# The channel products of a four-layer convolution kernel: one row per matmul on 64 partitions, in place of block-diagonal weights

## What is computed

```
layer 0:  q = x as (8, 64, 65536); att = q q^T; x = gamma * (softmax(max(att) - att) q) + x
layer 1:  x = conv2d(x, k1, separable 256x256 kernel per channel) + x * bias1
layer 2:  f1 = haar2d(x)
          for i in 0, 1:
              f4 = einsum('bchw,oc->bohw', f1 * v[i], conv_w[i])
              acc += sign(f4) * relu(|f4| - tau[i])
          x = haar2d_inverse(acc) + x
layer 3:  x = conv2d(x, k3) + x * bias3
```

## Time and profile before

| | |
|---|---|
| median of 3 runs | 6836.3 us (6832.41 to 6836.76) |
| the profiled execution's own time | 6835.24 us |
| its span in the trace | 6833.4 us |
| TensorE busy | 6388.9 us, 93% |
| VectorE, ScalarE, GpSimd busy | 65%, 58%, 39% |
| channel stage, eight times | about 240 us each, some 28% of the span |

### The profile page before, as it was taken

One profiled execution on the slowest core, in us unless ns is written; L12 is line 12 of the kernel. 1 busy time (PEld: TensorE's weight loads), 2 busy tenths in 40 slices (PEclk: granted clock), 3 DMA queues, 4 the chain that ended last, 5 costly groups with the idle time before them and its releaser, 6 DMA issues.

```text
span 6833.4 us, 144168 instructions
## 1 busy us (share of the span) xinstructions
PE 6388.9 (93%) x41056; PEld 5800.8 (85%) x41056; DVE 4433.1 (65%) x7037; ACT 3968.3 (58%) x5913; POOL 2698.2 (39%) x2052
## 2 busy tenths in 40 slices
PE   8998999889998899988999889998899988999689
PEld 7987999779997799977999779997799977998579
DVE  3667646676566764677646776567765677656766
ACT  1568545675456754567545775457654576545865
POOL 0149311483115831167311673117631176311852
PEclk9999999999999999999999999999999999999999
DMA  6654666546664466644666446664466644665236
GB/s 222 126 139 138 123 168 132 141 129 130 169 132 141 126 130 167 132 146 122 131 167 132 147 121 131 167 132 145 122 130 169 131 149 119 131 173 125 80 86 129
DMA packets 621293, 944.27 MB, mean 138 GB/s; under 512 B 62358, under 2 KB 456759, under 8 KB 621208
## 3 DMA queue, kind: packets, MB, share of 16 engines
q1 hardware_dynamic: 547480, 808.74, 51.3%
q10 hardware_dynamic: 73728, 134.25, 5.3%
HBM read 673.92 MB, written 268.83 MB: 138 GB/s over the span
## 4 chain that ended last, share of the span: by engine, by line
PE 75%; DVE 10%; ACT 8%; issue 3%; DMA 2%; POOL 1%; DVEq 1%; SPq 0%; ACTq 0%; POOLq 0%
PE ps L359 26%; PE ps L361 13%; PE ps L387 7%; PE ps L379 7%; PE ps L464 7%; PE ps L416 7%; PE ps L370 6%; DVE work L767 4%; DVE ps L782 4%; ACT ps L601 4%; ACT mag L598 4%; DMA work<-in_x_pix 1%; POOL mag L844 1%; PE ps L337 1%; DMA coef<-work 0%
## 5 line engine op out<-in xcount | busy, mean ns | idle before, releaser
L359 PE MATMUL ps<-work 128*128 128x256 f32 x8192 | 2455.2, 382 | 23.9 <-POOL work L833 16.3
L361 PEld LDWEIGHTS ps<-work 128*128 128x128 f32 x8192 | 1561.8, 191 | 214.3
L361 PE MATMUL ps<-work 128*128 128x128 f32 x8192 | 1578.0, 274 | 0.0
L359 PEld LDWEIGHTS ps<-work 128*128 128x128 f32 x8192 | 1315.8, 192 | 121.5 <-issue 20.7
L833 POOL COPY work<-field 128x512 f32 (+1 forms) x512 | 312.8, 614 | 2308.6 <-DVE ps L731 1623.3
L844 POOL TENSOR_TENSOR mag<-mag,sgn 128x1024 f32<-128x1024 f32 x512 | 1091.8, 2132 | 331.9 <-ACT mag L598 315.6
L862 POOL TENSOR_TENSOR split_a<-field,split_a 128x512 fp32r<-128x512 f32 x512 | 650.8, 1271 | 1418.8 <-ACT split_a L616 1418.8
L782 DVE TENSOR_TENSOR ps<-ps,tau_t 128x1024 f32<-128x1024 f32 x512 | 631.2, 1233 | 313.0 <-ACT ps L601 313.0
L569 ACT ACTIVATE work<-ps 128x512 f32<-128x512 f32 x512 | 306.1, 598 | 874.0 <-PE ps L361 871.1
L616 ACT ACTIVATE split_a<-field 128x512 fp32r (+1 forms) x512 | 322.9, 631 | 698.9 <-PE ps L379 694.6
L767 DVE TENSOR_TENSOR work<-ps,v_t 128x1024 f32<-128x1024 f32 x512 | 622.3, 1215 | 92.9 <-PE ps L464 92.9
(11 more groups left out here) (76 smaller groups left out, 9942.9 us busy)
## 6 DMA issues: line engine op xcount, KB each, us to landing
work<-filt SPq DMA_DIRECT2D x2048, 128.0 KB, 4.0
work<-in_x_pix SPq DMA_DIRECT2D x256, 512.0 KB, 5.4
coef<-work ACTq DMA_DIRECT2D x512, 256.0 KB, 2.1
out<-work SPq DMA_DIRECT2D x512, 256.0 KB, 4.1
rows<-in_x_rows SPq DMA_DIRECT2D x128, 512.0 KB, 4.4
mag<-in_x_rows SPq DMA_DIRECT2D x128, 512.0 KB, 4.4
rows<-coef SPq DMA_DIRECT2D x128, 512.0 KB, 3.6
split_a<-coef SPq DMA_DIRECT2D x64, 512.0 KB, 3.7
```

Source lines behind the costliest of these rows:

```text
L359: nc.tensor.matmul(o_ps, src[:, 0, H * half:H * half + H], tab[:, N - 1::-1], start=True, stop=False)
L361: mm = nc.tensor.matmul(o_ps[:, H:N], src[:, 1, H * half:H * half + H], tab[:, N - 1:H - 1:-1], start=False, stop=True)
```

## The change

The weights are no longer block-diagonal: `chan_w` holds the 64 x 128 weights twice, in partitions 0 to 63 and 64 to 127. The partitions of a chunk are ordered (s, c) in place of (c, s), so a matmul takes the 64 partitions of one half and 128 moving columns; there are eight of them in a unit, the lower and the upper half in turn, and half s writes bank 2(d%2)+s. The transposes write their columns in the new order; the tables `v` and `tau`, their views on VectorE, and the views of GpSimd's addition follow the new order of the banks. What each engine computes per unit is otherwise the same.

```diff
-        chan_w = sb("chan_w", [128, 4 * C])
+        chan_w = sb("chan_w", [128, 2 * C])
...
-                chunks = coef.rearrange("c (s t) n -> (c s) (t n)", s=2)
+                chunks = coef.rearrange("c (s t) n -> s c (t n)", s=2)
...
-                    sp.dma_start(crows[buf], chunks[:, bass.ds(1024 * k, 1024)]).then_inc(crows_in[buf], 16)
+                    sp.dma_start(crows[buf], chunks[:, :, bass.ds(1024 * k, 1024)]).then_inc(crows_in[buf], 16)
...
                     for a in range(2):
-                        o_ps = ps[:, 2 * (d % 2) + a, :].rearrange("p (i c h) -> p i c h", i=2, h=4)
                         for t in range(2):
                             at = 512 * t + N * a + H * (d % 2)
-                            mm = nc.tensor.matmul(o_ps[:, :, :, 2 * t:2 * t + 2], src[:, at:at + H], chan_w[:, :],
-                                                  start=True, stop=True)
+                            for s in range(2):
+                                o_ps = ps[:, 2 * (d % 2) + s, :].rearrange("p (a n t) -> p a n t", a=2, t=2)
+                                mm = nc.tensor.matmul(o_ps[:, a, :, t], src[C * s:C * s + C, at:at + H],
+                                                      chan_w[C * s:C * s + C, :], start=True, stop=True)
...
-                            mm = nc.tensor.transpose(o_ps[:, :, 2 * t:2 * t + 2], src[:, at:at + H], eye[:, :])
+                            turned = o_ps[:, :, 2 * t:2 * t + 2].rearrange("p c s -> p s c")
+                            mm = nc.tensor.transpose(turned, src[:, at:at + H], eye[:, :])
...
-                        at = t[:, j % 2, bass.ds(2 * q + j // 2, 1), :].rearrange("p o (x h) -> p (o x) h", h=4)
-                        return at.unsqueeze(2).to_broadcast([128, 4, C, 4])
+                        at = t[:, j % 2, bass.ds(2 * q + j // 2, 1), :].rearrange("p o (x h) -> p (o x) h", h=2)
+                        return at.unsqueeze(2).to_broadcast([128, 8, C, 2])
...
-                        both = mag[:, d].rearrange("p (a i n) -> p a i n", a=2, i=2)
-                        nc.gpsimd.tensor_tensor(pair_sum[:, d].rearrange("p (a n) -> p a n", a=2),
-                                                both[:, :, 0, :], both[:, :, 1, :], ALU.add)\
+                        both = mag[:, d].rearrange("p (s a i n) -> p s a i n", s=2, a=2, i=2)
+                        nc.gpsimd.tensor_tensor(pair_sum[:, d].rearrange("p (a n s) -> p s a n", a=2, s=2),
+                                                both[:, :, :, 0, :], both[:, :, :, 1, :], ALU.add)\
```

More of the change, by code:

```diff
@@ L766, in shrink @@
                         dve.wait_ge(c_sign, u - 1 + CR)
-                        nc.vector.tensor_tensor(held[:, j % 2].rearrange(grouped, x=4, h=4),
-                                                banks(j % 2).rearrange(grouped, x=4, h=4), table(v_t), ALU.mult)\
+                        nc.vector.tensor_tensor(held[:, j % 2].rearrange(grouped, x=8, h=2),
+                                                banks(j % 2).rearrange(grouped, x=8, h=2), table(v_t), ALU.mult)\
                             .then_inc(c_scaled, 1)
@@ L779, in shrink @@
                     if on[0]:
-                        less = banks(j % 2).rearrange(grouped, x=4, h=4)
+                        less = banks(j % 2).rearrange(grouped, x=8, h=2)
                         dve.wait_ge(c_abs, u + 1 + CR)
@@ L893, in per_pixel @@
         t = t.reshape(2, N, N)[:, order_h][:, :, order_w].reshape(2, 2, 2, CHUNKS, 2, 2, H)
-        return np.ascontiguousarray(t.transpose(6, 5, 3, 1, 0, 4, 2)).reshape(H, -1)
+        return np.ascontiguousarray(t.transpose(6, 5, 3, 2, 1, 0, 4)).reshape(H, -1)
     arrays["v"] = per_pixel(a["L2_conv_v"])
@@ L898, in layout @@
     cw = a["L2_conv_conv_w"].transpose(2, 0, 1).reshape(C, 2 * C)
[L899 to L902, removed]
+    arrays["cw"] = np.concatenate([cw] * 2, axis=0)
     t = np.linspace(0.0, 1.0, N)[::-1]
```

## The result

Before 6835.6 us (6832.41 to 6836.76, 4 runs), after 8053.9 us (8050.45 to 8060.31, 4 runs): the ratio is 1.178, 95% interval 1.176 to 1.181. 7910 was forecast, with a range of 7600 to 8650. The profiled execution of the changed kernel took 8050.45 us, its span 8048.6; that is 1215.2 more than before.

A forecast was written before the change was run, and what follows sets the result against it. GpSimd's 3.56 us a unit and the bank-pair chain were taken to bound the kernel. Loads on two engines add 140.0 us in each of seven stages and 99 in the last: 6835.2 + 1079 = 7914, given as 7910, range 7,600 to 8,650.

The forecast's parts named there:

- Loads on two engines: Channel stage's coefficient loads: source's outermost extent 2 puts each load on 2 DMA engines, 256 KB each.
- Rate of two engines alone: Coefficient loads: 26.0 GB/s per engine, 10.08 us a load against the 7.08 that the units need.
- Pix on the shared engines: Pix loads queued with coefficients in seven stages: 2.52 us per block on each engine; upper bound 3.23.
- Products: Channel stage's matmuls on TensorE: 1.99 us a unit becomes 1.05 if halves overlap fully, 2.10 if not.
- GpSimd's strided addition, VectorE's tables, transposes: Channel stage: all costed at nothing; the addition stays at 1.27 us, upper bound 2.13.
- TensorE waits about 4 us a chunk: Channel stage: products wait for coefficient loads, about 4 us idle per chunk; nothing added for TensorE slowing down.
- Landing over 20 us: Changed profile: median landing of the coefficient loads over 20 us.
- GpSimd's own limit: Channel stage: GpSimd needs 3.56 us a unit without gaps, so shorter products gain nothing in the steady state.
- the chain on one pair of banks: Channel stage: scale, abs, subtract, relu, products make 6.50 us, about 7.08 with gaps, for two units.
- Rival C: Loads don't slow, but unoverlapped products (+56 us) or GpSimd's strided write (up to +440) do: 6,890 to 7,275; chance 0.08.
- Rival D: Faster: loads on 16 engines, halves overlap, first products at eight starts save 15 us: about 6,810, -0.4%; chance 0.04.

The follow-up runs named there:

- experiment 1: Changed kernel with each chunk loaded by two DMAs of 64 channels in place of one nested DMA: 6867.8 us, ratio 1.0053.
- experiment 2: Kernel before with only the nested load, the rows of weights and transposes permuted to match: 8059.8 us (1 run).
- experiment 5: Changed kernel with only the first half of each pix block loaded, used twice by the Gram products: 7815.2 us (1 run).
- experiment 3: Changed kernel with each pix block loaded by one DMA of 1 MB in place of two of 512 KB: 8048.8 us (1 run).
- experiment 11: experiment 6 with GpSimd multiplying only one of the two banks by the sign: 6828.2 us, ratio 0.9996.
- experiment 12: Kernel before with GpSimd multiplying only one of the two banks by the sign: 6832.3 us, ratio 0.9998.
- experiment 9: experiment 6 with VectorE, not GpSimd, doing the pair addition of every fourth unit, two units late: 6850.8 us, ratio 1.0028.
- experiment 10: Kernel before with VectorE, not GpSimd, doing the pair addition of every fourth unit, two units late: 6857.6 us, ratio 1.0037.
- experiment 6: experiment 1 with the next batch's first pix blocks issued earlier, behind chunks 0 and 2: 6845.3 us, ratio 1.0013.

## Why the prediction was right, and where not

- **Loads on two engines: right.** It was the chosen reading of the earlier trace rows, and no row showed it. Now 20 small packets for ten loads do, with a flat 52 GB/s. Experiments 1 and 2 isolate it. The page has 617,717 packets, 3,576 fewer than before's 621,293; 3,584 were forecast, and 8 more packets of the instruction queue make up the difference. The Trainium skill ("DMA: Bandwidth & Descriptors", section "Why a DMA increments its semaphore by 16 and not by 1") takes the slowest dimension above 1 of both patterns and the largest number of engines up to 16 that divides both. These runs agree: 2 small packets a load with 2 outermost in the source, though 128 stand outermost in the output.
- **Rate of two engines alone: right.** 26.0 GB/s and 10.08 us a load were taken from the full stretches of the earlier trace rows; 26.3 and 9.98 were measured. The last batch's stage was forecast at 339.7 us and took 337.4.
- **Pix on the shared engines: the mis-sized term.** A block was costed at 2.52 us on each of the two engines, with the rate for 16 engines in full flow; the periods give 4.1, experiment 5 shows that it goes with the bytes, and experiment 3 excludes the number of starts. 16 blocks by 1.6 us are 25 a stage, less 3 from the slightly shorter loads: 22, against the measured 400.0 - 380.0 = 20.0. Seven stages make the 133 us by which 980 fell short of 1113, and almost all of the 144 between 7910 and 8053.9. That is beyond the 3.23 us that the prediction took as its upper bound from the 20.3 GB/s of the mix stage. Some 1.4 us of a block are coefficient packets that slow down beside pix, which the prediction put at nothing. The stage's share and rate came out accordingly, 0.24 and 84 GB/s for 0.2 and 90. Why a burst on all 16 engines moves more slowly than two engines alone is open.
- **Products: right in direction.** 1.05 to 2.10 us was the span; 1.16 was measured alternated, 1.71 apart, so alternated halves do overlap. At the low clock of a stage's start the unit's products fell from 3.78 to 2.08.
- **GpSimd's strided addition, VectorE's tables, transposes: nothing, right.** 1274 ns against 1271 for the addition, 1223 ns against 1.22 us for the scale. The upper bound of 2.13 us was far off.
- **TensorE waits about 4 us a chunk: right**, 3.7. It also slowed down in them: 2.08 us in place of 1.16 after a wait of 5.51, and a granted clock of 0.67 to 0.76 over the stages. This cost nothing that the runs show, as forecast: the last batch's 9.98 us a chunk are the two engines' own time. **Landing over 20 us** can't be read: the page gives no landing for these loads. What it does give is SyncE held for up to 12.8 us at an issue, where it was at most 0.5 for a coefficient load before, so some of the waiting in line seems to have happened on SyncE.
- **"GpSimd's own limit" of 3.56 us: wrong.** The sentence "GpSimd has no slack at all" rested on its being back to back with hardly a wait. Experiments 11 and 12 took 0.97 us a unit from it and the period stayed at 7.08. Back to back showed that GpSimd was one of several that took 3.54 us; it didn't show that it alone set it. The other limit named beside it, the chain on one pair of banks, falls with the same runs: in experiment 11 its products are 0.83 us shorter, with GpSimd relieved. Its "gaps" up to 7.08 us were waiting: in the earlier trace rows the products end at 1405.81, and the scale that reads them starts only at 1406.16, behind VectorE's subtraction. The conclusion drawn from it, that shorter products are worth nothing in the steady state, is right for another reason: what remains is the loop of VectorE and ScalarE. That is read from the timeline, after products and GpSimd were excluded by runs. Experiments 9 and 10 fit it, since VectorE took 0.68 us more in a unit that still lasted 3.54. But no run shortened the loop, so it isn't shown. Rival C, which priced a slower GpSimd from 3.56 us on, was not met, as GpSimd didn't slow.
- **Rival D, faster.** Its condition, loads that keep up and halves that overlap, is met in experiments 6 and 11. 6810 was its price, and they gave 6845 and, with part of GpSimd's work left out, 6828. Its 15 us from faster first products did not appear. SyncE's longer issues (a median of 0.48 us for each of the two 64-partition loads against 0.33 for one load before) and the longer wait for the first pix block stand at the same place; that they ate the 15 us is not shown. No version ran measurably faster than the kernel before.

## What to carry to other kernels

When a rearrangement changes the outermost extent of a DMA's pattern, count that extent before anything else: 2 in place of 128 cost 18% here with the same bytes and runs, and splitting it into one DMA for each half gave it back. A DMA share that sits flat at a multiple of 1/16 can be a few full engines and not an idle system; here it was two. And an engine without waits is a suspect, not a proof: lighten it alone and see if the period moves before you price any gain or loss against it.

## What the runs showed that I had not expected

- A pix block cost each of the two loaded engines 4.1 us for 65,536 bytes, a price of 15.9 GB/s, where an engine moved 26 when it and one other worked alone. Part of the price, about 1.4 us, lies in coefficient packets of 170 ns in place of 159.
- The issue of one coefficient load held SyncE for up to 12.8 us with two engines at work, and for at most 2.2 us in experiment 1 with 16. I read that as full queues; no run shows it. The 64-partition loads take 0.48 us each to issue, in the median.
- With the halves one after the other TensorE's records filled 150 of 150 us and the granted clock stayed at 0.50; alternated it was 0.76 with 100 us busy, and with the 128-partition products of before 1.00 with 102 us busy in the same stretch.
